# A macaron transformer block on Trainium2: projections, gate and up as three rounded whole-array products instead of fp32 column tiles

## What is computed

```python
def fp4_linear(x, w):                      # blocks of 16 along the last axis, rounded to an FP4 grid
    return jnp.einsum('bsk,nk->bsn', fp4_quant_dequant(x), fp4_quant_dequant(w))
def ffn(x):                                # w_gate, w_up: 352x128, w_down: 128x352
    return fp4_linear(silu(fp4_linear(x, w_gate)) * fp4_linear(x, w_up), w_down)
def attn(x):                               # 16 heads of 64
    q, k, v = split_heads(x @ w_q), split_heads(x @ w_k), split_heads(x @ w_v)
    o = softmax(q @ k.T * 64 ** -0.5) @ v
    return layernorm(merge(o) @ w_proj + b_proj + x, eps=1e-6) * gamma + beta
x = x + 0.5 * ffn(layernorm(x))
x = x + attn(layernorm(x))
x = x + 0.5 * ffn(layernorm(x))
```

## Time and profile before

| | |
|---|---|
| median of three runs | 2264.37 us |
| the profiled execution | 2263.16 us, of which the span is 2261.4 us |
| PE busy with matmuls | 2142.7 us (95% of the span) |
| DVE, POOL, ACT busy | 1605.5, 1407.7, 1151.4 us (71, 62, 51%) |
| the chain that ended last | PE 85%, DVE 6% |
| granted TensorE clock | 1.00 from 82 to 2200 us, 0.71 before, 0.67 after |

### The profile page before, as it was taken

How to read it: one execution, slowest core, us unless ns; L and a number is a source line. 1 busy time by engine, 2 the same in 40 slices (tenths; PEclk the granted TensorE clock), 3 DMA queues, 4 the chain that set the end, 5 groups by cost and what they waited for, 6 DMA issues and landing times.

```text
span 2261.4 us, 38387 instructions
## 1 busy us (share of the span) xinstructions
PE 2142.7 (95%) x14537; PEld 1094.4 (48%) x14537; DVE 1605.5 (71%) x2609; ACT 1151.4 (51%) x1749; POOL 1407.7 (62%) x1289
## 2 busy tenths in 40 slices
PE   3899999999999999999999999999999999999974
PEld 2344444545445454545545454554544545454432
DVE  5565767767687786868777686877778687776634
ACT  2455554645555454555545455455555545454532
POOL 3365666757576675757756576675757667665642
PEclk8799999999999999999999999999999999999986
DMA  1000000000000000000000000000000000000000
GB/s 60 1 7 2 6 2 2 12 2 7 7 7 7 2 11 2 7 7 7 7 2 11 2 7 7 2 12 2 10 3 6 7 2 12 2 2 7 2 7 10
DMA packets 167493, 15.83 MB, mean 7 GB/s; under 512 B 148304, under 2 KB 166928, under 8 KB 167312
## 3 DMA queue, kind: packets, MB, share of 16 engines
q1 hardware_dynamic: 167312, 13.39, 5.1%
HBM read 7.03 MB, written 4.19 MB: 5 GB/s over the span
## 4 chain that ended last, share of the span: by engine, by line
PE 85%; DVE 6%; SPq 2%; issue 2%; POOL 2%; DMA 1%; ACT 1%; POOLq 0%; DVEq 0%
PE pS L934 23%; PE pO L961 20%; PE pM L918 9%; PE pX L946 5%; PE pM L1077 5%; PE pX L985 5%; PE pM L973 3%; PE LpF L333 2%; PE FpF L333 2%; SPq L568 2%; PE FpF L296 2%; PE LpF L296 2%; PE LpF L309 2%; PE FpF L309 2%; PE LpF L324 1%
## 5 line engine op out<-in xcount | busy, mean ns | idle before, releaser
L676 POOL TENSOR_TENSOR ES<-ES,E 128x512 f32<-128x512 f32 x512 | 654.9, 1300 | 217.1 <-ACT E L747 209.9
L747 ACT ACTIVATE E<-pS 128x1024 f32<-128x1024 f32 x512 | 523.2, 1022 | 459.9 <-PE pS L934 421.3
L799 DVE TENSOR_REDUCE nmax<-pX 128x2 fp32r<-128x1024 f32 x512 | 622.0, 1215 | 113.4 <-PE pX L946 98.4
L961 PE MATMUL pO<-E,VA 128*64 128x512 f32 x2048 | 552.3, 618 | 0.0
L670 POOL TENSOR_TENSOR ES<-E 128x512 f32<-128x512 f32 x256 | 321.9, 1279 | 247.5 <-ACT E L747 247.5
L918 PE MATMUL pM<-xf,w_raw 128*64 128x512 f32 x1024 | 267.1, 600 | 2.8 <-DVE QL L889 2.1
L934 PE MATMUL pS<-QH,KH 64*128 64x512 f32 x1024 | 255.9, 496 | 0.0
L946 PE MATMUL pX<-KH,QH 64*128 64x512 f32 x1024 | 241.0, 412 | 4.7 <-DVE nmax L799 3.3
L934 PEld LDWEIGHTS pS<-QH,KH 64*128 64x128 f32 x1024 | 95.5, 183 | 288.1 <-issue 269.3
L946 PEld LDWEIGHTS pX<-KH,QH 64*128 64x128 f32 x1024 | 186.3, 306 | 36.7 <-DVE nmax L799 8.0
L934 PE MATMUL pS<-SH,onesr 64*128 64x512 f32 x1024 | 203.6, 393 | 0.0
(11 more groups left out here) (178 smaller groups left out, 3000.0 us busy)
## 6 DMA issues: line engine op xcount, KB each, us to landing
RROW<-RC SPq DMA_DIRECT2D x512, 2.0 KB, 2.0
xin<-in_L_attn_x SPq DMA_DIRECT2D x16, 256.0 KB, 3.0
SH<-nmax SPq DMA_DIRECT2D x256, 2.0 KB, 2.0
LC<-LROW SPq DMA_DIRECT2D x256, 2.0 KB, 2.1
out<-X SPq DMA_DIRECT2D x16, 256.0 KB, 2.5
w_raw<-in_L_attn_w_q SPq DMA_DIRECT2D x1, 512.0 KB, 3.6
w_raw<-in_L_attn_w_k SPq DMA_DIRECT2D x1, 512.0 KB, 4.7
w_raw<-in_L_attn_w_v SPq DMA_DIRECT2D x1, 512.0 KB, 5.6
```

What stands on the lines that cost most here:

```text
L676: ins = g.tensor_tensor(ES[i % 3][:, hd, :], ES[i % 3][:, hd, :], E[s][:, hd, :], ALU.add)
L747: a.activation(E[s][:, :, :], pS[:, :, :], ACT.Exp).then_inc(s_exp, 1)
L799: v.tensor_reduce(nmax[px % 2][:, :, t:t + 1], pX[:, :, :], AX.X, ALU.max, negate=True).then_inc(s_max, 1)
L961: ins = pe_.matmul(pO[half(hd), :], VA[of][:, kt, j * 128 + 64 * hd:j * 128 + 64 * hd + 64], E[kt][:, hd, :], start=kt == 0, stop=kt == KT ...
```

## The change

1. The operands of Q, K, V, gate and up are split once into a high part, rounded to fp32r, and a low part, the rest. Each fp32 product on two column tiles becomes three fp32r products on the whole array (high by high, high by low, low by high), added up in PSUM.
2. The low parts are made by DVE: the layers' inputs (`dve_x`, two per batch), the attention's input (`xf`, one per batch), and once the weights. `low_parts` stands behind the maxima of the quarter. Gate now waits for DVE's low part (`s_xlo`) where it waited for ACT's copy.
3. PE's order within a quarter puts like tiles together: row tiles, column tiles, whole array. `downs` and `row_sums` move ahead of Q, K and the layers; in the quarters with `project`, Q or K and the layers come first, and `times_v`, `project` and `downs` behind them.
4. To make room, Q, K and O have three buffers instead of four, `xf` one, and some buffers of the layers are shared. The raw weights land in the buffers of the exponentials.

```diff
+    def pe_rows(self, c, k, w):
+        rows = slice(k * 128, k * 128 + 128)
+        for n, (x, y) in enumerate(((0, 0), (0, 1), (1, 0))):
+            ins = self.nc.tensor.matmul(self.bank(c, k)[:, 0:FF], self.xq[x][:, rows], self.wgu[y][:, w, :],
+                                        start=n == 0, stop=n == 2)
+        return ins
     def pe_gate(self, pe, c, k):
         if k == 0:
-            pe.wait_ge(self.s_xqT, c + 1)
+            pe.wait_ge(self.s_xlo, c + 1)
         elif not self.apart(c):
             pe.wait_ge(self.s_silu, 4 * c + k)
-        for n in range(2):
-            ins = self.nc.tensor.matmul(self.bank(c, k)[half(n), 0:FF], self.xqT[:, k * 128 + 64 * n:k * 128 + 64 * n + 64],
-                                        self.wguT[:, 0, 0:FF], start=True, stop=True)
-        ins.then_inc(self.s_gate, 1)
+        self.pe_rows(c, k, 0).then_inc(self.s_gate, 1)
...
+    def dve_x(self, dve, c):
+        dve.wait_ge(self.s_xhi, c + 1)
+        self.nc.vector.tensor_tensor(self.xq[1][:, :], self.pF[:, :], self.xq[0][:, :].bitcast(F32),
+                                     ALU.subtract).then_inc(self.s_xlo, 1)
...
+                for k in range(2):
+                    dve.wait_ge(s_wT, k + 1)
+                    v.tensor_tensor(wgu[1][:, k, :], (pO, pM)[k][:, 0:FF], wgu[0][:, k, :].bitcast(F32),
+                                    ALU.subtract).then_inc(s_wTlo, 1)
...
+                def low_parts(b, t):
+                    for c in batch_at(FirstLayer, FirstLayer.turn_x + 1, b, t):
+                        F.dve_x(dve, c)
+                    for c in batch_at(FirstLayer, FirstLayer.xf, b, t):
+                        dve.wait_ge(s_xfhi, c + 1)
+                        v.tensor_tensor(xf[1][:, :], F.pF[:, :], xf[0][:, :].bitcast(F32), ALU.subtract).then_inc(s_xf, 1)
+                    for c in batch_at(LastLayer, LastLayer.turn_x + 1, b, t):
+                        L.dve_x(dve, c)
                 def first_ffn(b, t):
+                    for c in batch_at(FirstLayer, FirstLayer.down, b, t):
+                        if c == 0:
+                            for k in range(3):
+                                dve.wait_ge(s_whi, k + 1)
+                                v.tensor_tensor(W[1][:, k, :], raw[k], W[0][:, k, :].bitcast(F32), ALU.subtract).then_inc(s_wlo, 1)
...
-                def per_head(k, p, x):
-                    for hd in range(2):
-                        ins = pe_.matmul(pM[half(hd), :], w_raw[:, k, p * 128 + 64 * hd:p * 128 + 64 * hd + 64], x,
-                                         start=True, stop=True)
+                def both_heads(k, p):
+                    for n, (w, x) in enumerate(((0, 0), (0, 1), (1, 0))):
+                        ins = pe_.matmul(pM[:, :], W[w][:, k, p * 128:p * 128 + 128], xf[x][:, :], start=n == 0, stop=n == 2)
                     return ins
...
+                        projects = s == 1 and p % 2 == 1 and there(i - 4, NP)
                         if s == 0:
                             times_v(i - 1, (p - 1) % PAIRS, KT - 1)
-                        else:
+                        elif not projects:
                             times_v(i, p, s - 1)
+                        if s == 2 and p % 2 == 0 and there(i - 1, NP):
+                            row_sums(i)
+                        if not projects:
+                            downs(b, 4 * p + s)
...
                         first_ffn(b, 4 * p + s)
                         last_ffn(b, 4 * p + s)
-                        if s == 1 and p % 2 == 1 and there(i - 4, NP):
+                        if projects:
+                            times_v(i, p, s - 1)
                             project(i, p)
-                        if s == 2 and p % 2 == 0 and there(i - 1, NP):
-                            row_sums(i)
+                            downs(b, 4 * p + s)
```

More of the change, by code:

```diff
@@ L307, in pe_up @@
             pe.wait_ge(self.s_h, 4 * c + k)
[L308 to L311, removed]
+        self.pe_rows(c, k, 1).then_inc(self.s_up, 1)
     def pe_h(self, pe, c, k):
@@ L384, in dve_max_h @@
         dve.wait_ge(self.s_h, 4 * c + 2 * k + 2)
-        self.qh.maxima(self.nc, dve, 2 * c + k + self.w0, self.part(self.h, k), self.span(k))
+        self.qh.maxima(self.nc, dve, 2 * c + k + self.w0, self.part(k), self.span(k))
     def dve_round_x(self, dve, c):
@@ L391, in dve_round_h @@
     def dve_round_h(self, dve, c, k):
-        self.qh.round(self.nc, dve, 2 * c + k + self.w0, self.part(self.mag, k), self.part(self.h, k))
+        self.qh.round(self.nc, dve, 2 * c + k + self.w0, self.mag[:, 2 * (k % self.parts) * FF:2 * (k % self.parts + 1) * FF], self.part(k))
     def pool_divide_x(self, pool, c):
@@ L401, in pool_divide_h @@
     def pool_divide_h(self, pool, c, k):
-        self.qh.divide(self.nc, pool, 2 * c + k + self.w0, self.part(self.h, k), self.span(k))
+        self.qh.divide(self.nc, pool, 2 * c + k + self.w0, self.part(k), self.span(k))
     def pool_rescale_x(self, pool, c):
@@ L461, in make_program @@
         X2 = [m.sb(f"X2{i}", [128, T * D]) for i in range(2)]
[L462 to L466, removed]
+        xf = [m.sb(f"xf{k}", [128, S], F32R) for k in ("hi", "lo")]
+        QH = [m.sb(f"QH{i}", [128, S], F32R) for i in range(3)]
+        QL = [m.sb(f"QL{i}", [128, S], F32R) for i in range(3)]
+        KH = [m.sb(f"KH{i}", [128, S], F32R) for i in range(3)]
+        KL = [m.sb(f"KL{i}", [128, S], F32R) for i in range(3)]
         SH = [m.sb(f"SH{i}", [128, S], F32R) for i in range(2)]
@@ L470, in make_program @@
         ES = [m.sb(f"ES{i}", [128, 2, S]) for i in range(3)]
-        OT = [m.sb(f"OT{i}", [128, S]) for i in range(4)]
+        OT = [m.sb(f"OT{i}", [128, S]) for i in range(3)]
         ON = [m.sb(f"ON{i}", [128, S]) for i in range(2)]
@@ L506, in make_program @@
         s_xmT_ps = m.sem("s_xmT_ps")
+        s_xfhi = m.sem("s_xfhi")
         s_xf = m.sem("s_xf")
@@ L539, in make_program @@
         s_yacc = m.sem("s_yacc")
+        raw = [E[k][:, :, :].rearrange("p h n -> p (h n)") for k in range(3)]
+        wmag = VA[0][:, :, :].rearrange("p t n -> p (t n)")[:, 0:NW]
         with nc.Block() as block:
@@ L1002, in first_ffn @@
                         F.pe_h(pe, c, k)
-                    for c in batch_at(FirstLayer, FirstLayer.down, b, t):
-                        F.pe_down(pe, c)
                     for c in batch_at(FirstLayer, FirstLayer.turn_xm, b, t):
@@ L1022, in last_ffn, with downs @@
                         L.pe_h(pe, c, k)
+                def downs(b, t):
+                    for c in batch_at(FirstLayer, FirstLayer.down, b, t):
+                        F.pe_down(pe, c)
                     for c in batch_at(LastLayer, LastLayer.down, b, t):
@@ L1075, in body @@
                                 pe.wait_ge(s_xf, b + 2)
-                            for n in range(2):
-                                ins = pe_.matmul(pM[half(n), :], xf[xb][:, kt * 128 + 64 * n:kt * 128 + 64 * n + 64],
-                                                 w_raw[:, 2, of * S:of * S + S], start=True, stop=True)
+                            for n, (x, w) in enumerate(((0, 0), (0, 1), (1, 0))):
+                                ins = pe_.matmul(pM[:, :], xf[x][:, kt * 128:kt * 128 + 128],
+                                                 W[w][:, 2, of * S:of * S + S], start=n == 0, stop=n == 2)
                             ins.then_inc(s_v, 1)
```

104 lines of the change are left out of this document (58 added, 46 removed).

## The result

The changed kernel takes **2270.65 us** (median of 17 runs, 2267.02 to 2274.46), the kernel before 2263.57 in the same comparison (17 runs, 2261.82 to 2268.29). The ratio is 1.0026, interval 1.0019 to 1.0034: **0.3% slower**, where 0.7% faster was forecast. The time lies inside the range. The profiled execution has a span of 2267.9 us, 6.5 more than before.

The account below looks back on a forecast made before the run. PE's own instruction list was taken to bound the kernel: −54.7 us of list, +37.5 of waits and +1 at the end make −16.2, so 2248 us against the median of 2264.37, range 2227 to 2289.

Parts of the forecast that it names:

- The price of the product: On PE, a whole-array fp32r product costs 0.22 us for 512 columns and 0.153 for 352.
- the bounds: Limits on the 512-column product's price: 0.215 us from an fp32 pass below, 0.233 from the fp32r row-tile pair above.
- The rival of dear products: PE's products cost 0.233 us, or 0.187 with 352 columns, bound by weight load: 2289 us, chance 0.22.
- The kinds of tiles: On PE, more switches between row, column and whole-array tiles add 55.6 us; entering whole array 0.107, leaving 0.10.
- the prediction's sum: PE's list: 76.8 us less for Q, K, V, 33.5 less for gate and up, 55.6 more for tile kinds: −54.7.
- The waits: PE waits for DVE in quarters 29, 0 and 5, 2.5 us in each of 15 batches: 37.5 us.
- t = 29: Quarter 29: the last layer's gate waits 1.3 us for DVE's low part, made behind the maxima.
- t = 0: Quarter 0: the first layer's gate waits 0.8 us for DVE's low part, made behind the maxima.
- t = 5: Quarter 5: up of the first layer waits 0.7 us for h on DVE, net 0.4.
- what I cost at nothing: Low parts as DVE work, fewer buffers, earlier row_sums and DMA rows: taken as covered, 0 us.
- Serial loads: Rival on PE: some 1470 products each pay 0.107 us for an uncovered weight load: 2405 us, chance 0.04.
- The start: At the kernel's start, two low parts add 0.8 us each while slower-clock products shrink by 0.3 each; taken as 0.

Follow-up runs that it names:

- run 4: Against the changed kernel, each Q and K product of 512 columns made as two of 256: 2274.57 us, 1.0007 of the kernel before.
- run 3: Against the changed kernel, a fourth product, low by low, for Q, K and V: 2337.08 us, 1.0287 of the kernel before.
- run 11: Against the changed kernel, Q, K and V each as one fp32 whole-array matmul instead of three fp32r ones: 2320.74 us, 1.0264 of the kernel before.
- run 1: Against the changed kernel, DVE makes all low parts ahead of the quarter's maxima: 2258.56 us, 0.9946 of the kernel before.
- run 10: Three products in the old order, but times_v late in quarter 21 and quarter 0's low part ahead of the maxima: 2243.94 us, 0.9921 of the kernel before.
- run 2: The changed kernel's three products, but in the order of the kernel before: 2257.94 us, 0.9935 of the kernel before.
- run 8: Changed kernel with times_v first in quarters 5 and 29, row_sums late, downs early, low parts ahead of maxima: 2251.63 us, 0.9942 of the kernel before.
- run 5: The changed kernel again, unedited, in a later session: 2271.3 us, 1.0026 of the kernel before.
- run 12: As run 10, with the last layer's first maxima of h one quarter later: 2240.99 us, 0.9898 of the kernel before.

## Why the prediction was wrong, by its own steps

**The price of the product was mis-sized**; this is the step that failed. "I take 0.22 for 512 columns, and 0.153 for 352" measured 0.233 and 0.16. That makes 1152 × 0.013 = 15 us and 768 × 0.007 = 5 us, 20 of the 23 us by which 2271 misses 2248. The error lies in the choice between the bounds: L1038 cost 0.55 less 0.33, and the 0.33 of a last pair scatters from 0.31 to 0.33, so 0.22 was no better known than 0.24, while the bound from the same type and weights, 0.233, stood in the same rows 0.01 away. The rival of dear products named the right price for 512 columns and the wrong mechanism for 352: no load binds a product (run 4), and with 0.16 in place of 0.187 it would have added 20, not 41 us. Its type, not its width or its load, makes the product dearer than a quarter of an fp32 product (runs 3, 4, 11).

**The kinds of tiles** cost what was forecast: 0.107 in, 0.10 out. With the corrected products PE's list shrinks by −54.7 + 20.4 = −34.3 us by the prediction's sum; distances from start to start give an estimate of −30 to −35. The page's busy time shows −20.8 only, in part since in each quarter with a wait a product's recorded end runs into it.

**The waits** were right where they were named: t = 29 forecast 1.3, with 1.19 in the timeline, and the quarter grew by 1.25 (though the maxima are only some 0.57 of it, run 1); t = 0 forecast 0.8, measured 0.82 by taking it away (runs 1, 10); t = 5 forecast 0.4, the quarter grew by 0.46 and lost 0.36 with the old order. **A place was missing**: "what I cost at nothing" did not name `downs`, whose early place in t = 16 makes Q, QL and the maxima late and so lengthens quarter 18 by 0.63 us, 9 us in 15 batches (gone with the old order, kept with early `downs`, runs 2 and 8). Something went the other way too: V's first matmul waits 8.6 us for DVE and others, where it waited 14.8 before. Before and after:

```profile
L1077 PE MATMUL pM<-w_raw,xf 128*64 128x512 f32 x512 | 137.5, 613 | 14.8 <-DVE ON L880 12.7
L1127 PE MATMUL pM<-Whi,xfhi 128*128 128x512 f32 x128 | 59.8, 467 | 8.6 <-DVE ON L922 6.8
```

So the sum of the waits came out near the forecast 37.5, in part by luck: 9.0 us of growth in mid-kernel over a list 30 to 35 shorter make some 39 to 44.

**Serial loads** did not happen. The measured row is run 4's: whole-array products 0.117 us apart, each with a load recorded at 0.19. The Trainium skill (TensorE: Matmul & The Clock Gate, Part 3, "What overlaps and what doesn't") lets a load overlap only when the row group differs, and these have the same one; the measurement decides against it. The formula of that page's "Back-to-back issue gap", which the page gives for a single isolated matmul, gave an estimate of 0.216 and 0.149 for products that measure 0.233 and 0.16; it holds for a quarter of an fp32 product (0.213) within 2%, and not for fp32r.

**The start** was taken at 0. The first profile of the change has it 2.4 us shorter, the second (run 5) 0.6, so most of the 2.4 is scatter between executions. The end gained nothing.

With the right price alone the prediction's own sum is −34.3 + 37.5 + 1 = +4.2 us instead of −16.2: within 2.3 us of the span's +6.5. That it comes so near owes something to the missing place and V's shorter waits, which about cancel. The gain in PE's list was real, and was eaten by waits that the new order and the new dependency made. Run 10 shows how much: with the same products, nearly the old order and one low part moved, the kernel is 0.8% faster than before, and run 12 makes that 1.0%.

## What to carry to other kernels

On an engine that is bound by its list, price a new instruction by the nearest row of the same type, and treat a difference of two distances as no more exact than their scatter: 0.013 us times 1152 was nearly the whole forecast gain. When order is changed to save cost at the seams, add up what each moved step makes late on the engines that read it, as carefully as what it saves; here fewer seams (−11 us) cost some 28 us of waits (run 2's stretch of scores is 17 us shorter in spite of them). And cure a wait where it stands: moving the one low part of t = 0 was worth 12 us and cost nothing, moving all of them put a wait of 0.65 us into another quarter and let a late copy take back the gain in t = 29.

## What the hardware showed that was not expected

- An fp32r product takes 9% longer than a quarter of an fp32 one: 0.233 us for 512 columns and 0.117 for 256, against 0.213, at a granted clock of 1.00 (runs 4 and 11).
- One fp32 matmul on the whole array costs 0.853 us, about the same as the pair of column tiles (0.86).
- Small DVE instructions stretched to the length of a POOL addition of 128x512 beside them (two in 2.52 us): L162 on 128x4 elements took 1.27 us instead of 0.163, L202 on 128x32 took 1.32 instead of 0.17, and L156 took 1.30, 1.22 on average in the change too. The Trainium skill (SBUF — State Buffer, "SBUF: two separate sides") says of the port pair that the two engines share that it "is an **exclusive lock**, not a bandwidth split". This trace agrees in that 1323.08 + 1.30 and 1324.78 + 1.27 are within 0.05 us of the ends of an addition each, 1321.83 + 2.52 and 1324.75 + 1.25. The page names DVE operations with two SBUF inputs, as L156 has, or in a two-port mode; L162 and L202 have one input, and no run shows their mode. Which of these instructions is caught depends on when it meets the addition: one kernel has both lengths in one execution (L202 in the change, 0.17 and 1.32), so a wait can appear or vanish with a change that does not touch it.
